# Attention queries: squares for the norm on GpSimd from the SBUF copies, in place of ScalarE from PSUM

## What is computed

```
xn = layernorm(x, g_norm)
q  = (xn @ Wq) -> 16 heads of 64;   k, v = split(xn @ Wkv)   (one head, 64 each)
k, v = [null_k; k], [null_v; v]
q  = q / max(norm(q), 1e-12) * q_scale;   k likewise * k_scale
sim = 8 * q k^T + relative position bias + null bias, masked and causal
out = layernorm(softmax(sim) v @ Wout) * g_out
```

## Time and profile before

| | |
|---|---|
| median of three runs | 2487.56 us (2485.59 to 2491.07) |
| the profiled execution's own time | 2490.37 us |
| its span in the trace | 2488.6 us |
| TensorE busy, matmuls | 2344.3 us (94%) |
| VectorE busy | 1739.9 us (70%) |
| GpSimd busy | 1337.5 us (54%) |
| ScalarE busy | 1237.4 us (50%) |

### The profile page before, as it was taken

The page is one execution under the profiler, slowest core; times in us unless marked ns, Lnnn a source line. Parts: engine busy times, 40 slices in busy tenths (PEclk is TensorE's granted clock), DMA queues, the critical chain, the costliest instruction groups (busy, mean ns, idle before and its releaser), DMA issues. The chain is left out here.

```text
span 2488.6 us, 56588 instructions
## 1 busy us (share of the span) xinstructions
PE 2344.3 (94%) x20593; PEld 1818.2 (73%) x20593; DVE 1739.9 (70%) x4089; ACT 1237.4 (50%) x3133; POOL 1337.5 (54%) x1464
## 2 busy tenths in 40 slices
PE   5899999999999999889999999989899999999998
PEld 3677777777777777557777777757687877877876
DVE  4586777777777877578888887347674665755763
ACT  2676766666676766445555553124333333333332
POOL 3586777778786868266666666016332332322322
PEclk8999999999999999999999999999999999999999
DMA  4001210001010100011222212153111212111112
GB/s 147 18 27 30 64 40 28 27 28 34 22 36 27 29 23 23 22 23 40 49 57 58 57 38 57 39 163 94 39 60 44 73 56 60 55 58 60 60 35 61
DMA packets 192530, 122.10 MB, mean 49 GB/s; under 512 B 87728, under 2 KB 170672, under 8 KB 192256
## 3 DMA queue, kind: packets, MB, share of 16 engines
q1 hardware_dynamic: 166768, 79.74, 11.7%
q10 hardware_dynamic: 25488, 38.73, 5.2%
HBM read 97.29 MB, written 21.14 MB: 48 GB/s over the span
## 5 line engine op out<-in xcount | busy, mean ns | idle before, releaser
L1615 POOL TENSOR_TENSOR m_hid_part<-m_hid,m_hid_part 128x512 fp32r<-128x512 f32 x176 | 238.1, 1353 | 553.8 <-ACT m_hid_part L1524 550.5
L991 POOL TENSOR_TENSOR a_bm<-a_bias,a_mask_add 128x512 f32<-128x512 f32 (+3 forms) x512 | 438.2, 877 | 119.9 <-DVE a_nm L726 113.9
L902 ACT ACTIVATE a_S<-a_S,a_nm 128x512 f32<-128x512 f32 (+3 forms) x512 | 289.6, 566 | 231.6 <-DVE a_nm L726 226.9
L726 DVE CUSTOM_DVE_ANT_0 a_S<-a_S,a_bm,a_nsn 128x512 f32<-128x512 f32 (+3 forms) x512 | 276.4, 546 | 78.2 <-PE a_S L476 69.3
L1536 ACT ACTIVATE m_hid<-m_G 128x512 f32<-128x512 f32 x176 | 105.5, 599 | 390.1 <-PE m_G L1470 355.8
L476 PE MATMUL a_S<-a_kT,a_qT 128*128 128x384 f32 (+3 forms) x1024 | 284.6, 361 | 0.7 <-DVE a_nm L726 0.5
L1697 DVE TENSOR_TENSOR m_hid<-m_hid,m_U 128x512 f32<-128x512 f32 x176 | 121.1, 688 | 223.2 <-PE m_U L1470 189.6
L1487 PE MATMUL m_Y<-m_hid_part,m_down_high 128*128 128x512 f32 x704 | 256.5, 405 | 12.3 <-POOL m_hid_part L1615 11.5
L1470 PE MATMUL m_G<-m_in,m_gate_high 128*128 128x512 f32 x704 | 251.8, 398 | 0.9 <-POOL m_up_low L1609 0.9
L1470 PE MATMUL m_U<-m_in,m_up_high 128*128 128x512 f32 x704 | 250.7, 396 | 1.5 <-DVE m_hid L1697 1.2
L486 PE MATMUL a_T<-s_ident,a_S 128*128 128x128 f32 x1280 | 230.2, 278 | 19.4 <-ACT a_PT L911 15.4
(11 more groups left out here) (326 smaller groups left out, 5263.2 us busy)
## 6 DMA issues: line engine op xcount, KB each, us to landing
a_o<-s_weight_rows SPq DMA_DIRECT2D x128, 128.0 KB, 3.0
m_spread<-s_w ACTq DMA_DIRECT2D x64, 256.0 KB, 3.3
m_spread<-s_w ACTq DMA_DIRECT2D x128, 128.0 KB, 2.9
a_x<-in_x SPq DMA_DIRECT2D x32, 128.0 KB, 2.8
s_hT<-a_hT SPq DMA_DIRECT2D x32, 128.0 KB, 2.2
d_x<-in_x SPq DMA_DIRECT2D x8, 512.0 KB, 5.3
d_h<-s_hT SPq DMA_DIRECT2D x8, 512.0 KB, 5.6
s_xg<-d_xg SPq DMA_DIRECT2D x8, 512.0 KB, 3.1
```

Source lines behind the costliest of these rows:

```text
L726: dve.tensor_tensor_reduce(S[:, n % S_SLOTS, 0:w], SB[n % 2][:, 0:w], bm[:, n % BM_SLOTS, 0:w], -1.0, nsn[:, tile % 2, h:h + 1], ALU.add, ...
L902: act.activation(S[:, n % S_SLOTS, 0:w], S[:, n % S_SLOTS, 0:w], ACT.Exp, scale=-1.0, bias=nm[:, tile % 2, h:h + 1], accum_out=den[:, tile ...
L991: pool.tensor_tensor(bm[:, n % BM_SLOTS, 0:w], bias[:, h, L - w:L], mask_add[b % 2][:, 0:w], ALU.add).then_inc(s["bm_ready"], 1)
L1615: pool.tensor_tensor(hid_part[1][:, q % H_SLOTS], hid[:, q % G_SLOTS], hid_part[0][:, q % H_SLOTS].bitcast(F32), ALU.subtract).then_inc(hi ...
```

## The change

ScalarE no longer squares the query blocks. It copies each block to `qraw` as before. GpSimd gets two steps `q0`, `q1` that wait for the copy and for the last use of `sq`, and multiply `qraw` with itself into `sq`. VectorE's `ss` waits for both engines. ScalarE still squares the key.

```diff
@@ names
-                 "xnT_high", "xnT_low", "q_ready", "kv_ready", "sq_ready", "ss_ready", "rr_ready", "qn_ready",
+                 "xnT_high", "xnT_low", "q_ready", "kv_ready", "sq_ready", "q_squared", "ss_ready", "rr_ready", "qn_ready",
@@ drained(name, t, n)
-                    "q1": [(s["q_ready"], 2 * t + 2)], "kv": [(s["kv_ready"], 3 * t + 3), (s["sq_ready"], 3 * t + 3)],
+                    "q1": [(s["q_ready"], 2 * t + 2)], "kv": [(s["kv_ready"], 3 * t + 3), (s["sq_ready"], t + 1)],
@@ VectorE, "ss"
-                        dve.wait_ge(s["sq_ready"], 3 * (t + 1))
+                        dve.wait_ge(s["sq_ready"], t + 1)
+                        dve.wait_ge(s["q_squared"], 2 * (t + 1))
@@ ScalarE, "q0" and "q1"
-                        act.activation(sq[:, hs].rearrange("p a d -> p (a d)"), f[:, :], ACT.Square)\
-                           .then_inc(s["sq_ready"], 1)
                         act.copy(qraw[:, hs].rearrange("p a d -> p (a d)"), f[:, :]).then_inc(s["q_ready"], 1)
@@ GpSimd
+                    elif name in ("q0", "q1"):
+                        i = int(name[1])
+                        hs = slice(8 * i, 8 * i + 8)
+                        pool.wait_ge(s["q_ready"], 2 * t + 1 + i)
+                        if t > 0:
+                            pool.wait_ge(s["ss_ready"], t)
+                        pool.tensor_tensor(sq[:, hs], qraw[:, hs], qraw[:, hs], ALU.mult).then_inc(s["q_squared"], 1)
```

## The result

The changed kernel takes **2500.31 us** (median of 6, 2497.14 to 2506.51) where the kernel before took 2488.72 (6 runs, 2485.59 to 2491.07): ratio 1.0048, 95% interval 1.0034 to 1.0062. It is slower, inside the range, and 4.5 us above the predicted 2495.8. The profiled execution took 2497.67 us, span 2495.9, which is 7.3 us above the profiled execution before.

The account below looks back on a forecast made before the run. TensorE was taken as the bound, busy 899 of 949 us in the attention stage. Losses 3.2 + 4.8 + 0.7 - 0.5 = +8.2 us on the median 2487.56 gave 2495.8 us, range 2488 to 2505.

Parts of the forecast that it names:

- ScalarE's relief: Removing 64 squares (38.4 us) from ScalarE costed at nothing, except -0.5 us once for an earlier second copy in tile 0.
- The rival in which ScalarE's queue caused the late copies: Copies for head 2 or 3 come earlier; up to 15.4 us of TensorE waits won, half giving 2480; chance 0.10.
- The mechanism: VectorE's clamp after the reduction is held until GpSimd's running addition ends, delaying the next maximum, exponential, copy and transposes.
- some 23: Sign in the profile after: TensorE's waits for ScalarE's copies of transposed probabilities up from 15.4 to some 23 us.
- I take 1.26: Duration in us of each 128x512 GpSimd product, taken from additions with two full operands; 81 us in all.
- with a product of 1046 ns: Side case: last additions end 0.4 us earlier; 256 columns lose 0.1, 384 0.3, 512 0.5; +6 us.
- 0.1 for a 512-column tile: Loss in us where the clamp just gets in before the last addition and only the power is late.
- held in all three widths: Rival: the clamp meets the last addition in 512 columns too; +14.5 us, 2502; chance 0.25.
- the forecast's 8.2: Summed loss in us: eight 256-column tiles at 0.4, eight of 384 at 0.6, seven of 512 at 0.1, less 0.5.
- Passed on in full: The clamp's hold, 0.4 us in 256 and 0.6 in 384 columns, reaches TensorE whole through head 4's chain.
- costs nothing on top: In 384 columns GpSimd's power begins at 486.2 in place of 485.61, the clamp's same shift, adding no loss.
- L765 is not held: Rival: the clamp escapes the additions, only the late power counts, 0.3, 0.1, 0.1 a tile; +3.4 us, 2491; chance 0.17.

Follow-up runs that it names:

- e7: The change with the query squares left out altogether, on ScalarE and GpSimd, their part of `sq` holding ones: 2489.80 us.
- e4: The kernel before without VectorE's clamp of the sums (the maximum with 1e-24): 2483.30 us.
- e10: The kernel before with the clamp taken off VectorE and made by GpSimd right ahead of its power: 2489.12 us.
- e11: The change with the clamp taken off VectorE and made by GpSimd right ahead of its power: 2493.21 us.
- e5: The kernel before, ScalarE's squares kept, with the 64 products added on GpSimd and written to `qn`, used by nothing: 2501.98 us.
- e12: The change again, unaltered, timed beside other kernels: 2498.03 us, ratio 1.0036 to the kernel before.
- e2: The change with both products one head step later in GpSimd's queue, behind the addition for head 6: 2491.45 us.
- e8: The change with each product made twice on GpSimd, first into `qn`, then into `sq`: 2544.25 us.
- e1: The change with GpSimd's power one head step earlier in its queue, one addition less ahead of it: 2491.81 us.
- e3: The change without VectorE's clamp of the sums (the maximum with 1e-24): 2483.13 us.
- e9: The change with both moves in GpSimd's list, products one head step later and power one earlier: 2488.65 us, ratio 0.9997.
- e6: The kernel before with GpSimd's power one head step earlier in its queue: 2489.59 us, ratio 0.9999.

## Why the prediction was right, and where it was not

**ScalarE's relief is worth nothing but 0.5 us in tile 0: right.** Measured 0.55 in the change and 0.49 alone (e7). The rival in which ScalarE's queue caused the late copies is out: without the squares no tile but the first gains (e7), while taking the clamp's 0.18 us off VectorE shortens the 384-column tiles (e4, e10).

**The mechanism: right, and complete for two widths of three.** The clamp is held until the running addition ends, and TensorE waits 21.8 us for the copies (forecast: some 23). What none of the rows before showed, an odd length meeting an addition, is now shown: 17 columns, 0.41 to 0.86 us where they take 0.18. The reduction L765 keeps 1276 to 1290 ns beside the same additions; the Trainium skill (SBUF — State Buffer, "Who interferes with whom") says that a `tensor_reduce` never takes part in the lock on Trainium2, and by that rule the trace agrees.

**The step that failed: "I take 1.26" for a product.** It measured 1.04 us. The prediction had this case worked out ("with a product of 1046 ns"): 0.8 + 2.4 + 3.5 - 0.5 = +6. That side sum has a slip. It lets the additions end 0.4 us earlier in every width, which is the saving of two products. In 256 and 384 columns GpSimd waits for the second copy between the two products (the idle 0.31 and 0.35 in the rows above), so only the second one counts, 0.2: 256 loses 0.2 and 384 0.4. In 512 the two run back to back and 0.4 is right, which leaves 0.6. Done so, it reads 8 x 0.2 + 8 x 0.4 + 7 x 0.6 - 0.5 = +8.5, and the measured 0.24, 0.35 and 0.58 lie close to each of its terms.

**The second: 0.1 for a 512-column tile.** I had placed the clamp within 0.05 us of the start of the last addition and took it to get in just before. With products of 1.04 us it lies well inside and costs 0.58 a tile, 4.1 us in all in place of 0.7, half of the total. So the rival "held in all three widths" is what happened, at less than its price (+14.5), since its sizes were those of the long product. Errors of -1.3 (256), -2.0 (384) and +3.4 (512) cancel, which is why the sum came out at the forecast's 8.2. That agreement is luck.

**"Passed on in full", and "costs nothing on top" for the late power: right for two widths of three.** In 256 columns the power alone is enough for the loss: e11, where nothing is held, loses 0.45 with the power 0.44 late; e5 0.57 with 0.56. In the change the hold has made head 4 0.18 us late there, and the power brings it to 0.24 at head 7. In 512 the late power is free (e11 against e10: 0.00 with 0.67), in 384 nearly (e5: 0.10 with 0.77; e11 against e10: 0.26 with 0.48), and the hold costs. The prediction let the late power in 512 columns delay the maximum of head 7 by 0.4 us; it came 0.36 earlier, because the null scores were no longer held by `qn`, which its own trace showed and it had not looked at. The rival "L765 is not held" is refuted as an account of the change, but its figure of 0.3 a tile for 256 columns was nearer to the truth than my sentence.

**The rest of the measured 8.8 to 11.6 us** goes with a lower granted clock, which the prediction did not have. It does not follow the holds alone. A mean clock of 0.978 or less stands in 11 of 35 runs of kernels with products and holds (the change, e12, e2, e5, e8), in 9 of 43 with products and no hold (e1, e3, e9, e11), and in 9 of 132 without products (the kernel before, e4, e6, e7, e10); e5 has none in six. So the count points at the products on GpSimd more than at the holds. That is a count over kernels made for another question, and the cause stays open.

## What to carry to other kernels

Before moving work to an engine with room, ask what the engine that gives it up was late for: ScalarE waited 226 us for VectorE, so 32 us less work there bought nothing. On the engine that takes it, look at the end of the queue that gets pushed, and lay the other engines' short instructions against it: here one clamp of 0.18 us a tile, met by the last of four pushed additions, made the loss in two widths of three, a power that came late made it in the third, and moving either of two steps by one place in the list took most or all of it away from the tiles. Look at the holds that are there already, too: a shift can end one. An operation's duration is to be taken from the row with the same kinds of operands, and where an instruction lies within 0.1 us of a border, both sides belong in the sum.

## What the runs showed of the hardware

- A GpSimd `tensor_tensor` of 128x512 whose two inputs are the same tensor takes 1.04 us, as with a broadcast operand (1046 ns); with two different full tensors it takes 1.26 to 1.30.
- A VectorE `tensor_scalar` in place on 17 columns is held by GpSimd additions that run back to back: by one in the change (up to 0.86 us), by the end of one and two more in e8 (2.63). A `scalar_tensor_tensor` of 16 columns was held by `qn` already before the change (0.97 for 0.27). Starting 0.1 us ahead of the border between two of them, it got through in e5's 384-column tiles (0.18), and in e8 it was passed over by both that followed. What decides there is open. The Trainium skill (SBUF — State Buffer, "Who interferes with whom") has whoever issues first keep the pair for its whole instruction and the other blocked; here two more went ahead of a blocked one, on which it has nothing.
- The maximum (L726) and the reduction (L765) run beside the same additions at their usual length: 0.60 to 0.62 us for 384 columns and 1.28.
